# One head's pair sums move from GpSimd to TensorE, and the candidate adds from VectorE to GpSimd, in a fused attention and product-key kernel

## What is computed

```python
q = (xn @ w_q.T).reshape(b, n, 2, h, kd).transpose(2, 0, 1, 3, 4)
sim = jnp.einsum('pbnhd,hkpd->pbnhk', q, keys)
s, i = jax.lax.top_k(sim, k)
sx, sy = (s[0], s[1])
ix, iy = (i[0], i[1])
all_scores = (sx[..., :, None] + sy[..., None, :]).reshape(b, n, h, k * k)
all_idx = (ix[..., :, None] * nk + iy[..., None, :]).reshape(b, n, h, k * k)
scores, pk = jax.lax.top_k(all_scores, k)
idx = jnp.take_along_axis(all_idx, pk, axis=-1)
w_down = key_in[idx]
w_up = key_out[idx]
o = jnp.einsum('bnd,bnhkd->bnhk', inputs, w_down)
o = jax.nn.gelu(o, approximate=False) * jax.nn.softmax(scores, axis=-1)
return jnp.einsum('bnhk,bnhkd->bnd', o, w_up)
```

## Time and profile before

| what | value |
|---|---|
| median of 3 runs | 1811.86 us (1811.05 to 1820.54) |
| the profiled execution | 1817.61 us, span of its trace 1815.9 us |
| mean granted TensorE clock | 0.958 of full speed |
| TensorE, VectorE, ScalarE, GpSimd busy, 800 to 1800 us | 822, 896, 823, 950 us of 1000 |

### The profile page before, as it was taken

How to read it: one execution, slowest core, us unless ns; L and a number is a source line. 1 busy time by engine, 2 the same in 40 slices (tenths; PEclk the granted TensorE clock), 3 DMA queues, 4 the chain that set the end, 5 groups by cost and what they waited for, 6 DMA issues and landing times.

```text
span 1815.9 us, 37722 instructions
## 1 busy us (share of the span) xinstructions
PE 1536.1 (85%) x11712; PEld 1091.8 (60%) x11712; DVE 1481.7 (82%) x3720; ACT 1268.6 (70%) x1741; POOL 1332.3 (73%) x1579
## 2 busy tenths in 40 slices
PE   3899999999999999768887888878878788887877
PEld 2455555555556666346666766666666666666656
DVE  3668888788888887159899988989889898898988
ACT  1156666666666666558888878888888888788885
POOL 1045555555555555569999999999999999999993
PEclk9689999999999999879999998999999999999999
DMA  5334444443444442100000000000000000000000
GB/s 141 76 81 98 99 97 95 101 96 95 103 103 103 99 99 56 43 29 1 19 18 1 19 18 18 0 18 18 1 18 18 11 8 18 18 0 18 13 6 7
DMA packets 73406, 85.14 MB, mean 47 GB/s; under 512 B 9856, under 2 KB 63616, under 8 KB 68608
## 3 DMA queue, kind: packets, MB, share of 16 engines
q1 hardware_dynamic: 73312, 84.08, 19.7%
HBM read 58.10 MB, written 25.95 MB: 46 GB/s over the span
## 4 chain that ended last, share of the span: by engine, by line
POOL 24%; issue 19%; DVE 7%; ACT 5%; PE 1%; POOLq 0%; DVEq 0%; ACTq 0%; SPq 0%
POOL SUM L751 24%; DVE W L944 4%; ACT E L852 3%; ACT L786 1%; DVE M8Y L888 0%; PE WT L1012 0%; DVE SMALL L888 0%; DVE SMALL L905 0%; ACT GE L785 0%; DVE CT L927 0%; ACT SIM L779 0%; ACT BNT L794 0%; PE MB L979 0%; DVE Z L911 0%; PE E L967 0%
## 5 line engine op out<-in xcount | busy, mean ns | idle before, releaser
L751 POOL TENSOR_TENSOR SUM<-SIM 128x1024 f32<-128x1024 f32 x512 | 959.9, 1912 | 39.8 <-DVE W L944 36.1
L944 DVE SCALAR_TENSOR_TENSOR W<-SUM,SMALL,E 128x1024 f32<-128x1024 f32 x512 | 646.1, 1280 | 86.2 <-ACT E L852 82.1
L852 ACT ACTIVATE E<-SUM,NB 128x1024 f32<-128x1024 f32 x512 | 567.4, 1118 | 136.1 <-DVE W L944 121.6
L1012 PE MATMUL WT<-idf,W 128*128 128x128 f32 x4096 | 554.3, 285 | 104.2 <-DVE CT L927 53.5
L1012 PEld LDWEIGHTS WT<-idf,W 128*128 128x128 f32 x4096 | 476.3, 147 | 274.8 <-DVE W L944 143.0
L264 POOL TENSOR_SCALAR_AFFINE_SELECT PT<-PT 128x128 f32<-128x128 f32 (+1 forms) x1024 | 336.4, 353 | 323.4 <-ACT PT L354 287.2
L409 DVE TENSOR_REDUCE mx<-SX 128x2 f32<-128x512 f32 x256 | 175.4, 685 | 102.7 <-PE SX L492 102.0
L411 DVE TENSOR_REDUCE mx<-SY 128x2 f32<-128x768 f32 x256 | 242.7, 948 | 7.7 <-PE SY L492 7.3
L354 ACT ACTIVATE PT<-TX 128x512 f32<-128x512 f32 x256 | 152.8, 597 | 102.2 <-PE TX L519 100.9
L356 ACT ACTIVATE PT<-TY 128x768 f32<-128x768 f32 x256 | 207.0, 808 | 2.0 <-PE TY L519 0.8
L488 PE MATMUL SY<-K,Q 72*128 72x384 bf16 x512 | 164.0, 343 | 15.6 <-DVE mx L411 14.9
(11 more groups left out here) (111 smaller groups left out, 1671.1 us busy)
## 6 DMA issues: line engine op xcount, KB each, us to landing
K<-k_parts SPq DMA_DIRECT2D x96, 192.0 KB
Q<-q_parts SPq DMA_DIRECT2D x288, 64.0 KB
q_parts<-qp SPq DMA_DIRECT2D x16, 384.0 KB, 2.4
k_parts<-kp SPq DMA_DIRECT2D x16, 384.0 KB, 2.4
xin<-in_x SPq DMA_DIRECT2D x16, 256.0 KB, 3.1
xres<-in_x SPq DMA_DIRECT2D x16, 256.0 KB, 9.0
x<-X SPq DMA_DIRECT2D x16, 256.0 KB, 2.3
x2T<-X2T SPq DMA_DIRECT2D x16, 256.0 KB, 2.1
```

Source lines behind the costliest of these rows:

```text
L751: return eng.tensor_tensor(SUM[(q * FH + h) % RING][:, :].rearrange("p (i j) -> p i j", i=NK), sx, sy, ALU.add)
L852: nc.scalar.activation(E[h % 2][:, :], SUM[(k * FH + h) % RING][:, :], ACT.Exp, bias=NB[q][:, h:h + 1]).then_inc(S["exp_ready"], 1)
L944: nc.vector.scalar_tensor_tensor(out=W[h % WRING][:, :], in0=SUM[(k * FH + h) % RING][:, :], scalar=TOP[q][:, h, TOPK - 1:TOPK], in1=E[h % ...
L1012: o = pe.matmul(WT[:, e, :], W[h % WRING][:, e * P:(e + 1) * P], ident[:, :], is_transpose=True, start=(h == 0 and e % 4 == 0), stop=(h == ...
```

## The change

TensorE makes the pair sums of head 4 (`PEH`). For that, the scores of heads 4 and 5 of tile j + 1 are turned in MB before the outputs (`turn_sims`, in tile j), ScalarE copies the 64 rows of head 4 to SIMT before the output copy (`simT_copy`), and in the next tile TensorE multiplies SIMT by PAIRS, a matrix of ones and zeros of 64 x 1024 with two ones in a column, straight into E0 (`pe_sums`). ScalarE's exponential of head 4 reads E0 and writes W, and VectorE's mask of head 4 reads both and writes W. SIM is stored head by head for this. The ring of SUM buffers has 14 in place of 16.

GpSimd makes the sums of the seven other heads, and before head 2 of each tile the candidates of the next, in two adds (28 candidates in place of 20). It waits there for the searches of tile j + 1 and for the subtraction of tile j. The 16 MAX8 of a tile are done two tiles ahead: in tiles k = 0 and 2 all before the mask of head 4, in tiles k = 1 and 3 four each before heads 0, 2, 3 and 5. Their results now lie in SBUF.

```diff
+EVEN_RANKS = (0, 0, 0, 0, 16, 0, 0, 0)
+ODD_RANKS = (4, 0, 4, 4, 0, 4, 0, 0)
+TOP_AT, SUM_AT, BIAS_AT = 4, 6, 7
...
+        def candidates(j, q):
+
+            pool.wait_ge(S["ranked"], j + 1)
+            wait_pos(pool, S["top_less_max"], j)
+            x, y = M8X[q], M8Y[q]
+            nc.gpsimd.tensor_tensor(CD[:, :, 0:16].rearrange("p h (a b) -> p h a b", a=2),
+                                    x[:, :, 0:2].unsqueeze(3).broadcast_to([P, FH, 2, 8]),
+                                    y[:, :, :].unsqueeze(2).broadcast_to([P, FH, 2, 8]), ALU.add)
+            nc.gpsimd.tensor_tensor(CD[:, :, 16:28].rearrange("p h (a b) -> p h a b", a=6),
+                                    x[:, :, 2:8].unsqueeze(3).broadcast_to([P, FH, 6, 2]),
+                                    y[:, :, 0:2].unsqueeze(2).broadcast_to([P, FH, 6, 2]), ALU.add).then_inc(S["candidates"], 1)
...
                 for h in range(FH):
+                    if h == 2 and (more or k < GT - 1):
+                        candidates(j + 1, (k + 1) % 2)
+                    if h == PEH:
+                        continue
                     sum_buffer_free(pool, j, h)
...
+        def simT_copy(j, k):
+
+            act.wait_ge(S["sim_turned"], j + 1)
+            wait_pos(act, S["pe_sums"], j - 1)
+            nc.scalar.copy(SIMT[k % 2][:, :], MB[0:2 * NK, P:2 * P]).then_inc(S["simT_copied"], 1)
...
+                    if h == COPY_OUT and nxt:
+                        simT_copy(j + 1, k + 1)
...
+                    if h == PEH:
+                        act.wait_ge(S["pe_sums"], j + 1)
+                        wait_pos(act, S["weights_turned"], j * FH + h - WRING + 1)
+                        nc.scalar.activation(W[h % WRING][:, :], E[h % 2][:, :], ACT.Exp, bias=NB[q][:, h:h + 1]).then_inc(S["exp_ready"], 1)
...
+        def turn_sims(j, k):
+
+            pe.matmul(MB[:, P:2 * P], SIM[k % 4][:, PEH:PEH + 2, :, :].rearrange("p h a k -> p (h a k)"), ident[:, :],
+                      is_transpose=True, start=True, stop=True).then_inc(S["sim_turned"], 1)
+
+        def pe_sums(j, k):
+
+            for u in range(2):
+                o = pe.matmul(E[PEH % 2][:, u * GN:(u + 1) * GN], SIMT[k % 2][:, :], PAIRS[:, u * GN:(u + 1) * GN], start=True, stop=True)
+            o.then_inc(S["pe_sums"], 1)
...
+                    if h == SLOT_OUT and (more or k < GT - 1):
+                        turn_sims(j + 1, k + 1)
                     if h == SLOT_OUT and real:
                         outputs(j - 1, *((g, b, k - 1) if k else (g - 1, 1 - b, GT - 1)))
...
                     pe.wait_ge(S["weights_masked"], j * FH + h + 1)
 
+                    if h == PEH - 2:
+                        pe.wait_ge(S["simT_copied"], j + 1)
+                        pe_sums(j, k)
```

More of the change, by code:

```diff
@@ L582, in step @@
                     for g in range(2 * FH):
-                        o = pe.matmul(mb[:, g * NK:(g + 1) * NK], WQF[:, g, :], KT[:, g * NK:(g + 1) * NK], start=True, stop=True)
+                        at = (g % FH * 2 + g // FH) * NK
+                        o = pe.matmul(mb[:, at:at + NK], WQF[:, g, :], KT[:, g * NK:(g + 1) * NK], start=True, stop=True)
                     o.then_inc(S["keys_merged"], 1)
@@ L672, in ffn @@
     OUT = [sb(f"OUT{b}", [P, GT, P]) for b in range(2)]
-    SIM = [sb(f"SIM{b}", [P, 2, FH, NK]) for b in range(4)]
+    SIM = [sb(f"SIM{b}", [P, FH, 2, NK]) for b in range(4)]
+    M8X = [sb(f"M8X{b}", [P, FH, TOPK]) for b in range(2)]
     M8Y = [sb(f"M8Y{b}", [P, FH, TOPK]) for b in range(2)]
@@ L683, in ffn @@
     CT = [sb(f"CT{b}", [P, BLK, P]) for b in range(2)]
+    SIMT = [sb(f"SIMT{b}", [2 * NK, P]) for b in range(2)]
+    PAIRS = sb("PAIRS", [2 * NK, NE])
     E = [ps(f"E{b}", [P, NE]) for b in range(2)]
@@ new lines, in rank, with tops @@
+            for e in range(first, first + count):
+                to = M8X[q] if e < FH else M8Y[q]
+                o = nc.vector.max(to[:, e % FH, :], SIM[r][:, e % FH, e // FH, :])
+            if first + count == 2 * FH:
+                o.then_inc(S["ranked"], 1)
+        def tops(j, q):
+            await_(dve, S["candidates"], j + 1)
+            for h in range(FH):
+                o = nc.vector.max(TOP[q][:, h, :], CD[:, h, :])
+            o.then_inc(S["top_ready"], 1)
+            dve.wait_ge(S["top_ready"], j + 1)
+            nc.vector.tensor_tensor(D8[:, :, :], TOP[q][:, :, :], CD[:, :, 0:1].broadcast_to([P, FH, TOPK]), ALU.subtract).then_inc(S["top_less_max"], 1)
@@ L917, in _, with exp_sum, bias @@
+        def exp_sum(j):
+            dve.wait_ge(S["top_exp"], j + 1)
+            nc.vector.tensor_reduce(Z[:, :], E8[:, :, :], AX.X, ALU.add).then_inc(S["exp_sum"], 1)
+        def bias(j, q):
+            dve.wait_ge(S["log_sum"], j + 1)
+            nc.vector.scalar_tensor_tensor(out=NB[q][:, :], in0=LZ[:, :], scalar=-1.0, in1=TOP[q][:, :, 0], op0=ALU.mult, op1=ALU.subtract).then_inc(S["bias_ready"], 1)
         dve.wait_ge(S["x2T_loaded"], 16)
         nc.vector.tensor_scalar(BNT[0][:, :], X2T[0][:, :], ab[:, 0:1], ab[:, 1:2], ALU.mult, ALU.add).then_inc(S["bn_rows"], 1)
-        for part in range(8):
-            choose(part, 0, 0, 0)
+        rank(0, 0, 0, 0, 2 * FH)
@@ L922, in experts @@
+        tops(0, 0)
+        exp_sum(0)
+        bias(0, 0)
+        rank(1, 1, 1, 0, 2 * FH)
         def experts(j, g, b, k):
@@ L935, in group @@
                 for h in range(FH):
-                    if more or k < GT - 1:
-                        for part in (EVEN if k % 2 else BURST)[h]:
-                            choose(part, j + 1, (k + 1) % 4, 1 - q)
+                    ranks = ODD_RANKS if k % 2 else EVEN_RANKS
+                    if ranks[h] and (more or k < GT - 2):
+                        rank(j + 2, (k + 2) % 4, q, sum(ranks[:h]), ranks[h])
+                    if h == TOP_AT and (more or k < GT - 1):
+                        tops(j + 1, 1 - q)
+                    if h == SUM_AT and (more or k < GT - 1):
+                        exp_sum(j + 1)
+                    if h == BIAS_AT and (more or k < GT - 1):
+                        bias(j + 1, 1 - q)
                     if h == 1 and real:
@@ L992, in group @@
                         o_block(1 - b, 2 * k)
[L993 removed]
+                    if h == SLOT_OUT:
                         pe.wait_ge(S["sim_copied"], j + 3 if more or k < 2 else GROUPS * GT)
```

86 lines of the change are left out of this document (37 added, 49 removed).

## The result

| | before | changed |
|---|---|---|
| median of the runs | 1811.86 us (3 runs, 1811.05 to 1820.54) | 1886.16 us (4 runs, 1883.69 to 1893.22) |
| span of the profiled execution | 1815.9 us | 1884.3 us |
| start of the first mask | 800.8 us | 801.6 us |
| first mask to last mask | 1006.3 us | 1073.9 us |

The ratio of the changed kernel to the one before is 1.0393, with a 95% interval of 1.0374 to 1.0412: slower by 68 us between the two profiled executions and by 74 us between the medians. The forecast was 1875 us, in a range of 1843 to 1900. A fourth execution of the kernel before took 1967.81 us and counts as a slow one, so it is in neither the table nor the ratio.

What follows compares the result with a forecast made beforehand. The bound was taken to be the ScalarE-VectorE loop through two E buffers. 30 pairs x (1.61 + 0.14) = 52.5, plus 5 clock, 5 end, 1 start = 63.5 us on the 1811.9 median: 1875 us, range 1843 to 1900.

Steps and rivals of the forecast that it cites:

- What bounds the kernel: Memory stage: the ScalarE-VectorE loop through two E buffers binds, 15.6 us per tile; not GpSimd, busy 950 of 1000 us.
- The rival by which GpSimd was the bound: Memory stage: each tile falls by 0.9 to 1.4 us, 77 us in all, giving 1735 us; chance 0.03.
- The odd tile: Tiles k = 1 and 3: late TensorE sums delay mask 4 by 1.22 us, four MAX8 add 0.39; +1.61 us per tile.
- The signs: Odd tiles: exponential 4 waits about 2 us, mask 4 idle 2.2, odd-to-odd 33.4 and 32.7; GpSimd idle 1 to 3 per tile.
- That nothing catches up behind mask 4: Odd tiles after mask 4: four MAX8 add 0.39 us, the old chain follows, ScalarE's two copies hide in 0.1 to 0.6.
- The even tile: Tiles k = 0 and 2: sums hidden under gelu with 0.8 us to spare; copy to SIMT costs +0.14 us per tile.
- GpSimd: Seven sums 13.2 us plus two adds of 0.5 each; against a 16.5 us beat it still has room.
- Clock: TensorE's path from CT to the sums at half clock, about 8% of the time: 7.6 us, taken as 5.
- Start and end: Before the first mask two more ScalarE steps and 16 MAX8, +1 us; last three tiles about 5 us together.
- The sum: Whole kernel: 30 pairs x (1.61 + 0.14) = 52.5, plus 5 + 5 + 1, gives 63.5 us.

Runs made afterwards that it cites:

- early8: Kernel before, with 8 of the 16 MAX8 that odd tiles do for the next even tile done one tile earlier, before mask 4; 1803.0 us, ratio 0.994.
- candidates_only: Changed kernel without pair sums on TensorE: GpSimd makes all eight sums and the candidates, early searches stay; 1805.7 us, 0.997 of the kernel before.
- ranks_in_wait: Changed kernel with the four MAX8 of odd tiles before head 5 moved before head 4; 1877.1 us, 1.036 of the kernel before.
- pe_sums_only: Changed kernel with only TensorE's pair sums kept; candidates and searches as in the kernel before; 1880.7 us, 1.038 of the kernel before.
- double_sums: Changed kernel with each of the two pair-sum matmuls done twice; 1973.9 us (one run).
- half_sums: Changed kernel with one of the two pair-sum matmuls left out; 1850.1 us, 1.022 of the kernel before.
- outputs_third: Changed kernel with outputs and turn of the scores one head later, and the output copy ahead of the copy to SIMT; 1891.8 us, ratio to before 1.043.
- even_only: Changed kernel with TensorE's sums only in tiles k = 0 and 2, GpSimd making all eight in the others; 1796.1 us, 0.990 of the kernel before.
- even_shifted: Changed kernel, TensorE's sums in even tiles only, 8 odd-tile MAX8 moved into the even tile before, odd tile's candidates made at its head 0; 1772.1 us, ratio to before 0.976.
- even_shifted12: even_shifted with 12 instead of 8 of the odd tile's MAX8 moved into the even tile; 1765.0 us, 0.974 of the kernel before.

## Why the prediction was right, point by point

**What bounds the kernel: right.** The step from busy share to waits decided it. GpSimd, busiest at 95%, lost an eighth of its sums, and the stage became 7% longer. early8 shows the reverse: its time fell by a new order of VectorE's work alone. And in candidates_only GpSimd got more to do, up to being busy all the time, and the kernel was not slower. The rival by which GpSimd was the bound gave 1735 us. The rule of the Trainium skill (Perfetto Trace Analysis, Identifying the Most-Contended Engine) to shorten the engine of highest occupancy first is contradicted by these numbers: here it names an engine for which ScalarE waited 6.4 us.

**The odd tile: right in mechanism, 0.23 us too small.** Forecast +1.61 per odd tile over the 14.24 of the tile that I read; measured 16.08, so +1.84. Mask 4 starts 10.13 us after mask 0, where the working gave 9.88. The pieces: from the first load of the outputs to that of the sums it is 2.21 us (1431.07 to 1433.28) where I had 2.01, and exponential 4 started 0.12 behind the sums' end where I allowed 0.05; the sums themselves took 1.98 from their first load, as worked out (1.96). The four MAX8 at head 5 added their 0.39 in full. The sum over all 30 odd tiles is nevertheless close, 49.6 against 48.3, which is luck too: many odd tiles of the kernel before took 14.5 rather than 14.24.

**The signs.** Mask 4 was idle 2.41 us where I had put 2.2, odd-to-odd distances are 33.6 and 32.8 us where I had 33.4 and 32.7, and GpSimd's idle time at the candidates is 3.0 us per tile on average, at the end of the 1 to 3, nearly all of it in odd tiles (28 waits of 5.9 us). One sign was mis-sized: exponential 4 waits 4.14 us for TensorE and not about 2. ScalarE stands still from the end of exponential 3 (1431.24); in the tile of before that I followed this end is at 1394.00, 3.8 us ahead of the 1397.83 that I had worked out, so the longer wait was there to be read. About 2 is what VectorE loses.

**That nothing catches up behind mask 4: right, with a limit I had not seen.** I wrote that ScalarE's two copies hide there. They do only while the four MAX8 stand behind mask 4; with these away, exponential 5 holds mask 5, and 0.14 of the 0.39 us is not to be had (ranks_in_wait, pe_sums_only).

**The even tile: right, and cheaper than forecast.** +0.05 for the copy instead of +0.14. The 0.66 us that VectorE saved there were worth nothing, as forecast. The cover over the sums was 0.4 us (double_sums), where I had 0.8: in a tile k = 0 the sums end 8.96 us after mask 0 and not 8.75, exponential 4 starts at 9.47 and not 9.53, and 0.12 goes between the two.

**GpSimd: right.** The two adds took 0.42 and 0.36 us, against the 0.5 that I took. By the Trainium skill (GPSIMD Engine Reference, 3.1) the larger one would be 0.28, an estimate; this case measured half as much again. GpSimd's wait for the searches, up to 7.7 us, stayed free but at one place: in the first tile GpSimd stopped at the candidates with two sums made, and ScalarE waited 2.08 us for the third.

**The first tile: missed.** It took 17.19 us instead of 14.44, and GpSimd's stop is the smaller part. This tile has no gelu that could hide the pair sums, TensorE's granted clock is 0.50 from 803 to 811 us, the sums take 3.78 us there, and exponential 4 waits for them. These are lines of the changed kernel's first tile:

```profile
804.41 1.12 ACT L901 ACTIVATE E<-SUM,NB 128x1024 f32<-128x1024 f32 x1 [2.08 <-POOL SUM L765]
...
806.90 3.78 PE L1029 MATMUL E<-PAIRS,SIMT 64*128 64x512 f32 x4
...
810.71 1.11 ACT L897 ACTIVATE W<-E,NB 128x1024 f32<-128x1024 f32 x1 [3.32 <-PE E L1029]
```

With the sums on TensorE alone (pe_sums_only) this tile takes 16.50 us, with the candidates alone 15.46. Neither cost was in my sum.

**Clock: the term fell away where I had put it.** I put 5 us on TensorE's slow stretches among the odd tiles. Odd tiles of the loop, away from its turns, all took 16.08. What half clock cost lies in the first tile and behind the turns of the loop. The granted clock averages 0.99 over 800 to 1860 us, against 0.96 before.

**Start and end: right in size**, +0.8 and +5.6 against +1 and +5.

**The turns of the loop: missed.** +8.3 us. The sum was 63.5 us forecast against 68.4 between the two profiled spans: the first tile and the turns of the loop would be 11 more, the clock 5 less, and the even tiles 3 less. That the total is this close is thus in part luck, as misses of both signs partly cancel. The mechanism is not: it is that of the odd tiles, three quarters of the sum.

## What to carry to other kernels

An engine that is 95% busy and waits for others at the end of its ring is not the bound; look at who waits for whom before taking work off it. When work moves to an engine that runs in order, ask what stands ahead of it there and when the taker needs it: the same 2 us of matmuls alone cost 1.6 us per tile behind the outputs (pe_sums_only, 15.83 against 14.24) and nothing under gelu, so place them by tile, not everywhere. And work removed ahead of a late arrival is not a gain but a cover lost; a place where an engine waits anyway is where its other work should go.

## What the runs showed of the hardware

At a turn of the loop, TensorE of the changed kernel stood still for about 3 us without a semaphore to wait for, and what followed ran at half clock. Timeline of the changed kernel around a turn:

```profile
1475.76 0.86 PEld L1087 LDWEIGHTS WT<-idf,W 128*128 128x128 f32 x8 [0.58 <-DVE W L996]
...
1479.98 0.30 PEld L1009 LDWEIGHTS MB<-X2T,KI 128*128 128x128 f32 x2 [3.36 <-issue]
...
1481.35 3.18 PE L1087 MATMUL WT<-idf,W 128*128 128x128 f32 x16
...
1481.60 0.59 ACT L825 COPY GE<-MB 128x512 f32<-128x512 f32 x1 [1.51 <-PE MB L1009]
...
1483.32 1.29 DVE L996 SCALAR_TENSOR_TENSOR W<-SUM,SMALL,E 128x1024 f32<-128x1024 f32 x1 [0.87 <-PE WT L1087]
```

The expert block comes after 3.36 us of standing still, ScalarE's copy of it waits 1.51, the 16 turns take 3.18 us where 2.19 is usual, and VectorE waits 0.87 for them. Busy times, granted clock (the third number from the end) and DMA of that stretch and of the turns in it:

```profile
1472.00:1485.00 13.00, 9.05 (x51) 7.09 (x51) 9.69 (x15) 8.96 (x12) 13.00 (x8) 0.87 0.03 8
1481.00:1484.00 3.00, 3.00 (x14) 2.65 (x13) 2.13 (x3) 2.39 (x3) 3.00 (x3) 0.51 0.00 0
```

In the kernel before the same turn costs VectorE some 2 us in the tile ahead of it and nothing more. Behind it, pe_sums_only loses 3 us per turn and half_sums, which differs from the changed kernel by one matmul, nothing. The page counts 82 and 89 packets of instructions on two queues (q8 and q14) in the changed kernel, 36 and 58 before. The runs tell the two apart. Four kernels have this stop at all five turns from 900 us on: the changed one, pe_sums_only, ranks_in_wait and outputs_third; just these four have 82 packets on q8. The other nine have 36 or 37 there and no such stop, though half_sums, double_sums, even_only, even_shifted and even_shifted12 have 89 on q14 too. So the stop goes with the packets on q8, and not with those on q14 or with how many instructions are run, of which double_sums has the most. Whether loading them causes it, and what sets their number, stays open.

The granted clock was higher where TensorE had more to do: 0.96 over 800 to 1800 us before, with 822 us of TensorE busy, and 0.99 over 800 to 1860 us in the changed kernel, with 935. All runs fall in line: from 850 us to near the end the clock is 0.98 to 1.00 in the nine kernels with pair sums on TensorE, and 0.94 to 0.96 in the four without. half_sums and double_sums, which differ from the changed kernel in TensorE's work alone, have 0.99 and 1.00. Why the clock differs between the two sets stays open.
